# Attention's output packed raw and divided in place, with the reciprocals spread by a transfer

## The reference

```python
def _L0_attn_ref(x, w_q, w_k, w_v, w_o):
    HEADS = 32
    D_K = HIDDEN // HEADS
    def proj(w):
        y = jnp.einsum('bsd,ed->bse', x, w)
        return y.reshape(B, S, HEADS, D_K).transpose(0, 2, 1, 3)
    q, k, v = (proj(w_q), proj(w_k), proj(w_v))
    scores = jnp.einsum('bhqd,bhkd->bhqk', q, k) / jnp.sqrt(jnp.float32(D_K))
    attn = jax.nn.softmax(scores, axis=-1)
    out = jnp.einsum('bhqk,bhkd->bhqd', attn, v)
    out = out.transpose(0, 2, 1, 3).reshape(B, S, HIDDEN)
    return jnp.einsum('bse,oe->bso', out, w_o)

x = x + _L0_attn_ref(_layernorm(x, axis=-1), L0_attn_w_q, L0_attn_w_k, L0_attn_w_v, L0_attn_w_o)
x = x + _L0_ffn_ref(_layernorm(x, axis=-1), L0_ffn_gate_w, L0_ffn_w1, L0_ffn_w2, L0_ffn_w3)
```

## Time and profile before

| | |
|---|---|
| median of 3 runs | 637.93 us (635.51 to 640.77) |
| the profiled execution | 642.03 us, span 640.3 us |
| mean granted clock of TensorE in it | 0.942 of 2.4 GHz |
| PE busy | 587.1 us, 92% of the span |
| DVE busy | 385.6 us, 60% |
| ACT busy | 329.5 us, 51% |
| POOL busy | 121.0 us, 19% |
| DMA | 78.88 MB, mean 123 GB/s |

### The profile page before, as it was taken

The page is one execution under the profiler, slowest core; times in us unless marked ns, Lnnn a source line. Parts: engine busy times, 40 slices in busy tenths (PEclk is TensorE's granted clock), DMA queues, the critical chain, the costliest instruction groups (busy, mean ns, idle before and its releaser), DMA issues.

```text
span 640.3 us, 10494 instructions
## 1 busy us (share of the span) xinstructions
PE 587.1 (92%) x3585; PEld 434.8 (68%) x3585; DVE 385.6 (60%) x689; ACT 329.5 (51%) x481; POOL 121.0 (19%) x137
## 2 busy tenths in 40 slices
PE   2999999979999999999954999999999999998993
PEld 2886663334333333323753999999999999998982
DVE  6715657958999999614546682837465555647140
ACT  5222116846777777862215464737464646565330
POOL 5000111000101101101004003324150607060312
PEclk9899997968999999999855999999999999999898
DMA  8180336764756620043742555666666574843213
GB/s 316 61 98 1 50 50 84 107 70 71 99 69 93 85 79 18 13 150 116 303 179 70 212 182 160 180 203 165 213 161 228 108 282 76 312 70 120 25 14 38
DMA packets 29497, 78.88 MB, mean 123 GB/s; under 512 B 8490, under 2 KB 8746, under 8 KB 24859
## 3 DMA queue, kind: packets, MB, share of 16 engines
q1 hardware_dynamic: 24474, 68.84, 40.0%
q0 software_dynamic: 4992, 9.64, 8.8%
HBM read 58.64 MB, written 9.80 MB: 107 GB/s over the span
## 4 chain that ended last, share of the span: by engine, by line
PE 45%; issue 28%; POOL 9%; DVE 7%; ACT 4%; DMA 3%; SPq 2%; POOLq 1%; ACTq 0%
PE ps_o L590 9%; PE ps L609 6%; PE ps L578 5%; PE ps L579 4%; PE ps L580 4%; DVE neg_max L1106 4%; POOL out L540 4%; PE ps L665 3%; PE ps_m L609 3%; POOL xn L522 3%; PE ps L621 2%; PE ps_o L729 2%; ACT probs_t L934 2%; SPq L357 1%; DMA rec_row<-sum_rec 1%
## 5 line engine op out<-in xcount | busy, mean ns | idle before, releaser
L934 ACT ACTIVATE probs_t<-ps 128x1024 f32<-128x1024 f32 x128 | 124.0, 1023 | 44.4 <-PE ps L621 43.1
L578 PE MATMUL ps<-xgT_hi,w_hi 128*128 128x294 f32 (+1 forms) x416 | 127.0, 305 | 5.4 <-DVE xgT_lo L1282 2.9
L580 PE MATMUL ps<-xgT_hi,w_lo 128*128 128x294 f32 (+1 forms) x416 | 126.3, 304 | 0.0
L579 PE MATMUL ps<-xgT_lo,w_hi 128*128 128x294 f32 (+1 forms) x416 | 125.5, 302 | 0.0
L1106 DVE TENSOR_REDUCE neg_max<-ps 128x1 f32<-128x512 f32 x171 | 111.7, 684 | 13.5 <-PE ps L609 11.4
L1295 DVE TENSOR_TENSOR act<-gate,ps 128x294 f32<-128x294 f32 x48 | 22.1, 461 | 105.4 <-PE ps L580 86.8
L578 PEld LDWEIGHTS ps<-xgT_hi,w_hi 128*128 128x128 f32 (+1 forms) x416 | 79.0, 190 | 5.9 <-DVE xgT_lo L1282 3.2
L579 PEld LDWEIGHTS ps<-xgT_lo,w_hi 128*128 128x128 f32 (+1 forms) x416 | 78.7, 189 | 0.0
L580 PEld LDWEIGHTS ps<-xgT_hi,w_lo 128*128 128x128 f32 (+1 forms) x416 | 78.4, 188 | 0.0
L609 PE MATMUL ps<-k_stack,q_stack 48*128 48x512 f32 x171 | 74.9, 479 | 2.9 <-issue 0.3
L590 PE MATMUL ps_o<-probs_t,v_ones 128*32 128x512 f32 x512 | 72.3, 639 | 0.3 <-ACT probs_t L934 0.3
(11 more groups left out here) (249 smaller groups left out, 960.2 us busy)
## 6 DMA issues: line engine op xcount, KB each, us to landing
w_sb<-w SPq DMA_DIRECT2D x18, 1024.0 KB
w_sb<-w SPq DMA_DIRECT2D x9, 1536.0 KB
w_sb<-w SPq DMA_DIRECT2D x9, 1152.0 KB
q_stack<-q_hi SPq DMA_DIRECT2D x32, 128.0 KB, 5.1
k_stack<-k_hi SPq DMA_DIRECT2D x32, 128.0 KB, 4.8
q_stack<-q_lo SPq DMA_DIRECT2D x16, 128.0 KB, 4.9
k_stack<-k_lo SPq DMA_DIRECT2D x16, 128.0 KB, 5.9
q_hi<-o_norm SPq DMA_DIRECT2D x16, 128.0 KB, 2.9
```

The lines of the kernel that those rows point to most:

```text
L578: pe.matmul(o, x_hi, w_hi, start=start, stop=False)
L579: pe.matmul(o, x_hi, w_lo, start=False, stop=False)
L580: return pe.matmul(o, x_lo, w_hi, start=False, stop=stop)
L934: a.activation(probs_t[:, kc % 2, 2 * half:2 * half + 2, :], ps4[:, 2 * (n % 2):2 * (n % 2) + 2, :], ACT.Exp, scale=D ** -0.5).then_inc(s_ ...
```

## The change

After the change the pack takes the even partitions of `o_raw` itself, undivided, right behind the transfer of the sums, one step earlier than before. `rec_row` has four partitions, 0 to 3, and a new transfer at the end of the step (after the stacks, where the pack was) reads each of its rows sixteen times and writes the 64 partitions of `rec_all` that answer to the group's half of `o_all`. VectorE's shuffle is gone. POOL multiplies `o_all` by `rec_all` in place, once for two groups. The waits follow: the transfer into `rec_row` waits until the spread of the group before has landed (`s_sh`, now two semaphores of transfers), the spread waits for `rec_row` (`s_rb`) and for POOL's product of the pair before (`s_on`), `packed(n)` waits for POOL's products.

```diff
--- before.py
+++ after.py
@@ -89,7 +89,7 @@
         k0 = sb(att, "k_stack0", k_shape, f32r)
         v_ones = sb(att, "v_ones", [P, NT, NH, D, 2])
         sum_rec = sb(att, "sum_rec", [P, 2, GH * S // P])
-        rec_row = sb(att, "rec_row", [P, S])
+        rec_all = sb(att, "rec_all", [P, S])
         pro = ExitStack()
         w_hi, w_lo = zip(*((sb(pro, f"w{n}_hi", [P, HC, HID], f32r), sb(pro, f"w{n}_lo", [P, HC, HID], f32r))
                            for n in "qkv"))
@@ -108,8 +108,7 @@
         pro.close()
         probs_t = sb(att, "probs_t", [P, 2, GH, S])
         o_raw = sb(att, "o_raw", [P, 2, S])
-        rec_all = sb(att, "rec_all", [P, S])
-        o_norm = sb(att, "o_norm", [P, 2, S])
+        rec_row = sb(att, "rec_row", [GH, S])
         att.close()
         proj.close()
 
@@ -211,7 +210,7 @@
         s_so = [sem(f"s_so{r}") for r in range(2)]
         s_rc = sem("s_rc")
         s_rb = sem("s_rb")
-        s_sh = sem("s_sh")
+        s_sh = [sem(f"s_sh{r}") for r in range(2)]
         s_on = sem("s_on")
         s_oc = [sem(f"s_oc{r}") for r in range(2)]
         s_zero, s_zt = sem("s_zero"), sem("s_zt")
@@ -335,8 +334,8 @@
 
             sp.wait_ge(s_zero, 3)
             for m in range(SUBS):
-                sp.dma_start(out[T + m * P:T + (m + 1) * P, :], rec_row[:, :]).then_inc(s_init, 16)
-            sp.dma_start(xn2_dram[0:1, :], rec_row[0:1, :]).then_inc(s_rows, 16)
+                sp.dma_start(out[T + m * P:T + (m + 1) * P, :], rec_all[:, :]).then_inc(s_init, 16)
+            sp.dma_start(xn2_dram[0:1, :], rec_all[0:1, :]).then_inc(s_rows, 16)
 
             def ready(pair):
 
@@ -370,14 +369,16 @@
                 if 0 <= g < NG:
                     sp.wait_ge(s_rc, g + 1)
                     if g >= 1:
-                        sp.wait_ge(s_sh, g)
-                    sp.dma_start(rec_row[1:P:2 * D, :], sum_rec[:, g % 2, :]).then_inc(s_rb, 16)
+                        sp.wait_ge(s_sh[(g - 1) % 2], 16 * ((g - 1) // 2 + 1))
+                    sp.dma_start(rec_row[:, :], sum_rec[:, g % 2, :]).then_inc(s_rb, 16)
                 g = s - 1
                 if 0 <= g < NG:
                     sp.wait_ge(s_or, g + 1)
                     if g >= 2:
                         sp.wait_ge(s_rb, 16 * (g - 1))
                     sp.dma_start(sum_rec[:, g % 2, :], o_raw[1:P:2 * D, g % 2, :]).then_inc(s_so[g % 2], 16)
+                    sp.dma_start(o_all[64 * (g % 2):64 * (g % 2) + 64, g // 2, :],
+                                 o_raw[0:P:2, g % 2, :]).then_inc(s_oc[g % 2], 16)
                 if s in (-4, -3) or s >= 2:
                     pair = (s + 4) // 2 if s < 0 else (s + 6) // 2
                     if pair < NG // 2:
@@ -395,10 +396,15 @@
                     stack(1, range(2), "k")
                 g = s - 2
                 if g >= 0:
-                    sp.wait_ge(s_on, g + 1)
-                    sp.dma_start(o_all[64 * (g % 2):64 * (g % 2) + 64, g // 2, :],
-                                 o_norm[0:P:2, g % 2, :]).then_inc(s_oc[g % 2], 16)
-                if g == 8:
+                    sp.wait_ge(s_rb, 16 * (g + 1))
+                    if g < 2:
+                        sp.wait_ge(s_init, 16 * SUBS)
+                        sp.wait_ge(s_rows, 16)
+                    else:
+                        sp.wait_ge(s_on, g // 2)
+                    sp.dma_start(rec_all[64 * (g % 2):64 * (g % 2) + 64, :],
+                                 rec_row[:, :].unsqueeze(1).broadcast_to([GH, D, S])).then_inc(s_sh[g % 2], 16)
+                if s == 10:
                     sp.dma_start(wo_sb, wo.rearrange("p (c e) -> p c e", c=HC)).then_inc(s_wo, 16)
                     sp.dma_start(gw_sb[:, :, :], gw.rearrange("p (c e) -> p c e", c=HC)).then_inc(s_gw, 16)
                 if s in (NG - 2, NG - 1):
@@ -407,7 +413,7 @@
                     sp.dma_start(x1[:, b * TPB:(b + 1) * TPB, :], x_t[:, b * TPB:(b + 1) * TPB, :]).then_inc(s_x[b], 16)
 
             sp.wait_ge(s_pv, TPB * NG)
-            sp.wait_ge(s_on, NG)
+            sp.wait_ge(s_on, NG // 2)
 
 
 
@@ -467,7 +473,7 @@
         def _(pool):
             pool.memset(ident[:, :], 0.0).then_inc(s_zero, 1)
             pool.memset(before_b[:, :], 1.0).then_inc(s_zero, 1)
-            pool.memset(rec_row[:, :], 0.0).then_inc(s_zero, 1)
+            pool.memset(rec_all[:, :], 0.0).then_inc(s_zero, 1)
             pool.wait_ge(s_zero, 3)
             pool.affine_select(out=ident[:, :], in_=ident[:, :], compare_op=ALU.not_equal, fill=1.0,
                                base=0, pattern=[[-1, P]], channel_multiplier=1).then_inc(s_const, 1)
@@ -507,12 +513,11 @@
             pool.wait_ge(s_job, len(jobs))
             prepare(3)
 
-            for g in range(NG):
-                pool.wait_ge(s_sh, g + 1)
-                if g >= 2:
-                    pool.wait_ge(s_oc[g % 2], 16 * (g // 2))
-                pool.tensor_tensor(o_norm[:, g % 2, :], o_raw[:, g % 2, :], rec_all[:, :],
-                                   ALU.mult).then_inc(s_on, 1)
+            for pair in range(NG // 2):
+                for r in range(2):
+                    pool.wait_ge(s_oc[r], 16 * (pair + 1))
+                    pool.wait_ge(s_sh[r], 16 * (pair + 1))
+                pool.tensor_tensor(o_all[:, pair, :], o_all[:, pair, :], rec_all[:, :], ALU.mult).then_inc(s_on, 1)
             pool.wait_ge(s_pv, TPB * NG)
             pool.memset(w2_sb[:, FC - 1, :], 0.0).then_inc(s_tail, 1)
 
@@ -668,8 +673,7 @@
 
             def packed(n):
 
-                for r in range(2):
-                    pe.wait_ge(s_oc[r], 16 * n // 2)
+                pe.wait_ge(s_on, n // 2)
 
             def projection(t):
 
@@ -922,7 +926,7 @@
                         a.wait_ge(s_pv, TPB * (g + 1))
                         if g >= 2:
                             a.wait_ge(s_so[g % 2], 16 * (g // 2))
-                            a.wait_ge(s_on, g - 1)
+                            a.wait_ge(s_oc[g % 2], 16 * (g // 2))
                         a.activation(o_raw[:, g % 2, :], ps_o[:, :], ACT.Copy).then_inc(s_or, 1)
                     if 0 <= s < NG:
                         n = s * UNITS + u
@@ -1147,11 +1151,6 @@
                         v.reciprocal(sum_rec[:, g % 2, :], sum_rec[:, g % 2, :]).then_inc(s_rc, 1)
                         if s in (NG - 1, NG):
                             residual(s - (NG - 1))
-                    if u2 == 11 and g >= 0:
-                        v.wait_ge(s_rb, 16 * (g + 1))
-                        if g >= 1:
-                            v.wait_ge(s_on, g)
-                        v.stream_shuffle(rec_all[:, :], rec_row[:, :], [1] * 32).then_inc(s_sh, 1)
 
             for b in range(B):
                 for t in range(b * TPB, (b + 1) * TPB):
```

## The result

| | us, median (runs) | ratio to before, 95% interval |
|---|---|---|
| before | 637.43 (635.34 to 640.77, 14) | |
| changed | 643.66 (641.26 to 647.55, 14) | 1.0097 (1.0076 to 1.0119) |

The change makes the kernel 6.2 us slower. The forecast was 19.8 us slower, 657.7 us. The profiled execution of the changed kernel has a span of 645.8 us, that of before 640.3: 5.5 us between them.

The account below looks back on a forecast made before the run. TensorE and VectorE's exchange of banks bounds the 11.34 us step; afterwards SyncE's loop through the spread would. +20.3 (loop) - 1.0 (last shuffles) + 0.5 (end of attention) = +19.8 us on the 637.93 median: 657.7, range 632 to 670.

Parts of the forecast that it names:

- The step of 11.34 us and the 0.33 us of the shuffle: Attention's loop over groups: removing VectorE's shuffle saves 0.33 us a step, 11.34 becomes 11.0.
- The front: Step 2's late shuffle: stall and half clock cost 3.9 + 4.45 us; afterwards a 1.1 us stall at step 3's reciprocal.
- The loop through the spread: SyncE's queue: rec_row waits for the previous spread, making a loop of 11.15 us plus data time, above the engines' 11.0.
- 1.9 us of queue, and 1.2 us earlier it is 3.1: Queue time the spread finds behind the stacks, 3.1 us, added to its landing in SyncE's loop.
- s, the data time: Time the spread's 131,072 bytes need: 4.1 us chosen, at 32 GB/s; break-even 1.7 us.
- the narrow side over the engines: Spread's rate: four source partitions limit reads as narrow writes limit stacks, 4.1 us, rather than four engines' 1.2 us.
- The sum: Attention: spread 0, seven loops, then step 11's reciprocal at 253.6 against 233.3, +20.3; in all +19.8 us, 657.7.
- The clock: TensorE idling about 4 us a step may halve its clock; a last drop adds 4.45 us: 662, within the forecast's 0.75.
- The end of attention: Last spreads and POOL's product end at 308.9, TensorE needs the last chunk at 308.5: +0.5 us; expert weights add nothing.
- the last shuffles: Steps 11 to 13, after the stacks: three missing shuffles give back 1.0 us.
- Cheap as a pack: Rival: spread's data take 0.35 us, loop 11.5, time 627.2 us, 10.7 faster; chance 0.13.
- four engines at full rate: Rival: no narrow side, spread's data take 1.2 us, 3.9 us faster, 634.0 us, no difference that counts; chance 0.12.

Follow-up runs that it names:

- the best one: Changed kernel with reciprocal rows in partitions 0, 4, 8, 12, two buffers of them, and six stacks every step from step 1: 631.50 us, run again 627.37 us.
- no_shuffle: Kernel before with VectorE's shuffle left out and GpSimd multiplying by unspread rows, output not the reference's: 630.17 us, ratio 0.9871.
- even stacks: Kernel before, shuffle kept, issuing six stacks every step from step 1 instead of twelve in step 1: 630.15 us, ratio 0.9908; run again 631.35 us, 0.9918.
- smooth_after: Changed kernel with only the stacks issued otherwise, six in step 1 instead of twelve and later ones a step later: 642.23 us, ratio 1.0076.
- split: Changed kernel with the spread cut into four transfers of one source row each, rows still in partitions 0 to 3: 643.52 us, one execution.
- two_rows: Changed kernel with two buffers for the reciprocal rows, so SyncE waits for the spread of two groups before: 631.04 us, ratio 0.9868.
- spread_first: Changed kernel with the spread issued before the six stacks of its step instead of behind them: 660.79 us, ratio 1.0365.
- ports: Changed kernel with the reciprocal rows in partitions 0, 4, 8 and 12 instead of 0 to 3: 633.83 us, ratio 0.9935.

## Why the prediction was right and wrong

**The step of 11.34 us and the 0.33 us of the shuffle: right.** 11.01 measured in the changed kernel after 238, 11.03 without the shuffle, 11.01 in the best one.

**The front: right in the removal, and it missed a wait.** VectorE no longer waits at 130. But the prediction took the sums of group 1 as the only thing that is late next. The rows of maxima of group 3 stand in the same queue, behind the twelve stacks, and TensorE waits 2.35 us for them at 134.11. They had been late before as well, as `no_shuffle` shows, covered by the shuffle's 3.91 us. The even stacks take the wait away. The reciprocal of step 3 came at 135.95 instead of 133.8 to 134.9, and a short stretch at 1.2 GHz followed (1.93 us for eight value products). The loop hid this in the changed kernel: mending it changed the ratio from 1.0097 to 1.0076 (`smooth_after`), less than the intervals tell apart.

**The loop through the spread: right as a mechanism, 15.25 us forecast, 12.7 measured.** This is the step that failed, and in it one term: "1.9 us of queue, and 1.2 us earlier it is 3.1", added to the data time. Measured from issue to landing:

| spread | behind six stacks | alone |
|---|---|---|
| four neighbouring partitions | 6.8 | 6.8 |
| partitions 0, 4, 8, 12 | 6.1 | 3.3 |
| four neighbouring, as four transfers (`split`, from the first issue) | 6.9 | 6.4 |

The queue costs the wide spread 2.8 us, near the 3.1, and the narrow one nothing. The forecast had 9.45 for the narrow one behind stacks. The windows of `two_rows` fit that: the spread issued at 191.89 has 3 us behind the stacks, where its data take 5 alone, so a part of it probably ran beside them. The price of a narrow transfer at the end of a queue was the longer of the two, not their sum. `spread_first` shows an added delay where the order is turned round.

**s, the data time: 4.1 forecast, 4.55 to 5.2 measured.** 6.8 less the 2.25 of a landing is 4.55, and the windows at 25 to 27 GB/s give 4.9 to 5.2, which leaves 1.6 to 1.9 for the rest of the landing. The choice of the narrow side over the engines was right. The Trainium skill's page SBUF — State Buffer ("Door 1: The DMA port swizzle") gives 27.6 GB/s for partitions 0 to 3, which share one port, and puts 0, 4, 8 and 12 on four ports; the 25 to 27 and 104 GB/s here agree with it. The Trainium skill's page DMA: Bandwidth & Descriptors ("Why a DMA increments its semaphore by 16 and not by 1"), by which the spread gets four of the 16 engines, is borne out (the share was 0.19 to 0.27), but that limit was not the one that bound.

**The sum, with the measured terms.** The first spread was issued at 134.44, as forecast, and landed at 142.08 instead of 144.35 (2.3). Seven loops of 12.7 instead of 15.25 take 17.9 less. The `rec_row` transfer after the seventh went out at 232.81, where 251.1 was forecast: 18.3 less. Most of the 1.9 between that and the two terms is a loop of 14.0 us (206.06 to 220.10), in which the issue of a stack took 1.83 us. From there the reciprocal came 5.1 us later, where 2.5 was forecast, since most of that step ran at 1.2 GHz behind a gap of 3.44 us. So 237.91, +4.6 instead of +20.3.

**The clock: right as a risk.** Two gaps of TensorE (from 179 and from 217) each brought about a step at 1.2 GHz. The loop covers the first, the second is the 2.6 us just named.

**The end of attention: +0.5 forecast, +1.5 measured** (TensorE's wait at 313.85), less 0.9 for the last shuffles (1.0 forecast). The first expert's weights were asked for at 313.87 instead of 298.61, and ScalarE's wait for them stayed at 10.30 us after 10.32: hidden, as forecast. 4.6 - 0.9 + 1.5 = +5.2, the spans differ by 5.5.

**The rivals.** Cheap as a pack, and four engines at full rate, fall with the 25 GB/s of the spread, and `ports` and `split` say why. Only the place of the four rows decides the rate: with a stride of four the sum of the second of them nearly holds: a landing of 6.1 us behind stacks where its terms give 6.55 (3.1 + 2.25 + 1.2), a loop of 12.0 for 12.35, and 633.8 us for 634.0.

**What stays open.** Why a narrow transfer overlaps with the stacks ahead of it while the wide one behind them still costs 2.8 us, and what holds SyncE's next issue for 4.1 to 4.9 us. That hold is gone with the rows spread out (1.4 us) and also with the narrow source in four transfers (1.45 us), so in these runs it took both, the narrow source and the single transfer; the mechanism is not shown. The even stacks gained 5.2 to 5.9 us in the ratios and 8.4 us between the profiled executions (247.55 against 255.95 for the same reciprocal): the forecast took its 8.35 us of front from one execution of before, which ran 4.6 us over the median, and did not ask how much of that was the front. The executions differ ahead of the loop too: the clock stays at 1.2 GHz from 102 to 107 us in that of the changed kernel and to 119 in that of `ports`, whose reciprocal of step 2 comes 3.6 us later (126.33 after 122.70). Times at one place of two traces hold such differences; steps and landings do not.

## What to carry to other kernels

A wait in front of an issue on an in-order queue makes a loop of that issue and the landing it waits for. Add up that loop against the step first, and give the small buffer a second copy before anything else: here it was worth 2.3%. Rows that one transfer copies out many times moved four times as fast from partitions 0, 4, 8 and 12 as from 0 to 3. When pricing a transfer behind others, ask whether the queue's time and its own add or cover each other, and at which end of the queue it stands; and when a stall is removed, look for what else in the same queue was late beneath it.

## What was not expected of the hardware

- A source of four neighbouring partitions moved 25 GB/s with four engines and 25 to 27 GB/s with 13 to 14 busy ones; four partitions with a stride of four moved 104 GB/s with four engines.
- While such a transfer drains on four engines, SyncE's next issues are held: two rows of maxima took 4.8 to 4.9 us to issue instead of 1.4, a stack 4.1 to 4.5 instead of 0.6. Cut into four transfers, the same source held nothing (1.45).
- The same transfer lands 6.8 us after its issue behind six stacks and with the queue empty.
